# Graph attention on one core: the edge stage worked in pairs of units, with sums kept in four PSUM banks

## The reference

```
row, col = src, dst                                  # 212500 edges, 12500 nodes
xn = layernorm(h) * ln_w + ln_b                      # h = relu(layernorm(x)), H = 256
w_phys = (silu(rbf @ w1 + b1) @ w2 + b2) * cutoff[:, None]
msg_phys = xn[col] * w_phys
Q, K, V = xn @ wq + bq, xn @ wk + bk, xn @ wv + bv   # 8 heads of 32
scores = sum(Q[row] * K[col], -1) / sqrt(32) * cutoff[:, None]
attn = softmax(scores, axis=1)                       # over the 8 heads of an edge
combined = msg_phys + gate * (attn[..., None] * V[col])
aggr = segment_sum(combined, row)
out = x + h + aggr @ wo + bo
```

## Time and profile before

| | us |
|---|---|
| three executions, median | 6338.68 (6328.91 to 6351.49) |
| the profiled execution, its own time | 6347.99 |
| its span, first to last instruction | 6346.2 |
| PE busy | 5686.0 (90% of the span) |
| PEld busy | 4356.2 (69%) |
| DVE busy | 4708.3 (74%) |
| ACT busy | 3227.2 (51%) |
| POOL busy | 3783.6 (60%) |

### The profile page before, as it was taken

How to read it: one execution, slowest core, us unless ns; L and a number is a source line. 1 busy time by engine, 2 the same in 40 slices (tenths; PEclk the granted TensorE clock), 3 DMA queues, 4 the chain that set the end, 5 groups by cost and what they waited for, 6 DMA issues and landing times. The chain is left out here.

```text
span 6346.2 us, 114713 instructions
## 1 busy us (share of the span) xinstructions
PE 5686.0 (90%) x25995; PEld 4356.2 (69%) x25996; DVE 4708.3 (74%) x12728; ACT 3227.2 (51%) x12136; POOL 3783.6 (60%) x3580
## 2 busy tenths in 40 slices
PE   3689988889888888898799999999999999999999
PEld 3456655556555555565587787878888787788887
DVE  8588865555544444322599999999999999999995
ACT  4223322232322323222477777777777777777774
POOL 1466766666666566656666666666666666666660
PEclk9789999999999999998899999999999999999999
DMA  8433344334334433333698888988988888889835
GB/s 299 145 104 116 130 143 139 106 134 145 117 117 140 139 101 134 132 103 121 244 339 300 299 298 297 313 299 295 312 297 296 291 298 300 297 301 300 300 103 169
DMA packets 488176, 1350.47 MB, mean 213 GB/s; under 512 B 89614, under 2 KB 167222, under 8 KB 484858
## 3 DMA queue, kind: packets, MB, share of 16 engines
q0 software_dynamic: 230240, 900.22, 41.8%
q1 hardware_dynamic: 206904, 371.04, 18.1%
q10 hardware_dynamic: 50850, 77.03, 3.4%
HBM read 1074.68 MB, written 350.21 MB: 225 GB/s over the span
## 5 line engine op out<-in xcount | busy, mean ns | idle before, releaser
L937 POOL DMA_INDIRECT ukvx<-kvx_table,udst x1856 | 1946.4, 1049 | 1182.1 <-issue 534.8
L325 POOL DMA_INDIRECT records<-rows,slot_i x1660 | 1752.3, 1056 | 1141.6 <-DVE rows L574 522.6
L652 PE MATMUL w_ps<-w2s,hid 128*128 128x256 f32 x6656 | 1633.6, 400 | 226.7 <-DVE rows L574 203.3
L652 PEld LDWEIGHTS w_ps<-w2s,hid 128*128 128x128 f32 x6656 | 1289.6, 200 | 596.6 <-DVE rows L574 238.8
L758 ACT ACTIVATE hid<-hid_ps,b1t 128x512 f32<-128x512 f32 x832 | 525.7, 683 | 1888.7 <-PE hid_ps L641 964.3
L574 DVE TENSOR_TENSOR rows<-w_ps,b2b 128x512 f32<-128x512 f32 x832 | 569.0, 686 | 1196.4 <-remote 523.3
L1029 PE MATMUL uq_ps<-aggr,uonehotT 128*128 (+1 forms) x3712 | 1015.4, 396 | 95.0 <-issue 73.3
L1038 PE MATMUL ag_ps<-ukvx,uonehot_cut 128*128 128x256 f32 x3712 | 955.3, 380 | 0.1
L1041 PE MATMUL ag_ps<-ukvx,uonehot 128*128 128x256 f32 x3712 | 954.3, 380 | 0.0
L1038 PEld LDWEIGHTS ag_ps<-ukvx,uonehot_cut 128*128 128x128 f32 x3712 | 706.9, 190 | 97.0 <-issue 0.5
L1041 PEld LDWEIGHTS ag_ps<-ukvx,uonehot 128*128 128x128 f32 x3712 | 706.8, 190 | 96.5
(11 more groups left out here) (166 smaller groups left out, 6160.2 us busy)
## 6 DMA issues: line engine op xcount, KB each, us to landing
urec<-records SPq DMA_DIRECT2D x928, 260.0 KB
rbf_in<-in_edge_attr SPq DMA_DIRECT2D x207, 256.0 KB
kvx_table<-kvx ACTq DMA_DIRECT2D x10, 3456.0 KB
ukvx<-kvx_table,udst POOLq DMA_INDIRECT x1856
records<-rows,slot_i POOLq DMA_INDIRECT x1661
records<-kvx SPq DMA_DIRECT2D x1, 25480.0 KB
fbase<-x_plus_h SPq DMA_DIRECT2D x14, 896.0 KB, 7.1
out<-fout SPq DMA_DIRECT2D x13, 896.0 KB, 4.9
```

The costliest lines, as they stand in the source:

```text
L325: pool.indirect_dma_start(recs, bass.IndirectOffsetOnAxis(ap=slot_i[:, q, t:t + 1], axis=0), rows[:, q, t, :], None).then_inc(scattered[q] ...
L652: m = pe.matmul(w_ps[j % 2][:, h, :], hid[:, k % 2, c, h, j * P:(j + 1) * P], w2s[:, c, :], start=(h == 0 and c == 0), stop=(c == 1), skip ...
L937: pool.indirect_dma_start(kvx[:, k, j, :], None, table, bass.IndirectOffsetOnAxis(ap=dst_i[:, k, j:j + 1], axis=0), bounds_check=NPAD - 1, ...
```

## The change

- The unit of work in `edges` becomes a pair of units: four tiles, a ring of four pairs (RP) instead of eight units, 464 pairs. Instructions that took two tiles now take four where a PSUM bank allows it; the product of queries and keys stays in two halves.
- The sum stays in PSUM. Bucket b is summed in bank b mod 4. Ahead of each unit's sum PE writes zeros, with a bf16 product (L1070), into the bank after the one of the unit before. The identity product is gone. ACT copies the bank of bucket b - 2 to SBUF for both units of a pair (L1011), into the place that held that bucket's queries, and no longer writes zeros.
- The one-hots are made and transposed three pairs ahead, at the end of a pair's turn on DVE and PE. The gather goes three pairs ahead; its place is free when the pair before the present one has been summed.
- The normalised weights go to SBUF (`uattn`). The cutoff is copied out of the records (`ucut`, L974), so that SP waits for `phys_done`, `onehot_ready` and `dst_ready` before it loads a place anew.
- PE sums one pair behind instead of three units: filter products (`filtered`) between the two halves of the next pair's queries, the attention products (`attended`) after them.
- The first load of queries ahead of the records takes 7 buckets and not 28; the other 21 follow the first four loads of records. DVE instead of POOL clears the ring at the start.

PE, in the edge loop, one unit before. `uq_ps` are the queries, `ag_ps` the sums; the rows named ISA and REGISTER_ALU are instructions of PE's sequencer that put together addresses and counts.

The diff, cut to what the prediction speaks of:

```diff
-LAG = 3
+RP = DEPTH // 2
+BANKS = 4
...
+        GATHER_AHEAD, TURN_AHEAD, EVACUATE_AHEAD, QUERY_AHEAD, SUM_BEHIND, KEEP_BEHIND = 3, 3, 2, 1, 1, 1
...
-            sp.dma_start(aggr[:, QLAG:QLAG + QAHEAD * QC, :], q_v[:, 0:QAHEAD * QC, :]).then_inc(q_in, 16)
+            sp.dma_start(aggr[:, QLAG:QLAG + QC, :], q_v[:, 0:QC, :]).then_inc(q_in, 16)
...
+                    sp.wait_ge(s["phys_done"], v - (RP - 1))
+                    sp.wait_ge(s["onehot_ready"], v - (RP - 1))
+                    sp.wait_ge(s["dst_ready"], v - (RP - 1))
...
+                    pool.wait_ge(s["ag_done"], v - (RP - 1))
+                pool.wait_ge(s["dst_ready"], v + 1)
+                pool.sem_inc(s["dst_waited"], 1)
+                for j in range(4):
...
+            def keep(v, bucket, half):
+                if half == 0:
+                    if isinstance(v, int) and v == 0:
+                        act.wait_ge(s["zeroed"], 2)
+                    else:
+                        act.wait_ge(s["ag_done"], v)
+                        act.wait_ge(s["kept"], v)
+                else:
+                    act.wait_ge(s["half_kept"], v + 1)
+                act.activation(aggr[:, bass.ds(bucket + half, 1), :].rearrange("p a f -> p (a f)"), bank(bucket + (2 + half)),
+                               ACT.Copy).then_inc(s["half_kept" if half == 0 else "kept"], 1)
...
+            def turn(v, k, i, first):
+                pe.wait_ge(s["onehot_ready"], v + 1)
+                if not (isinstance(v, int) and v == 0):
+                    pe.wait_ge(s["ohT_ready"], v)
+                for j in range(4):
+                    m = pe.transpose(turn_ps[:, j, :], ohb[:, k, j, :], ident_bf[:])
+                m.then_inc(s["turned"], 1)
...
+                if half == 0:
+                    pe.wait_ge(s["ohT_ready"], v + 1)
+                    if not (first and k < 2):
+                        pe.wait_ge(s["qka_done"], v - 1)
+                elif not (isinstance(v, int) and v == 0):
+                    pe.wait_ge(s["qkb_done"], v)
...
+            def filtered(v, k, before, buckets):
+                if not (isinstance(v, int) and v == 0):
+                    pe.wait_ge(s["kept"], v)
+                pe.wait_ge(s["cut_ready"], v + 1)
+                pe.wait_ge(s["phys_done"], v + 1)
+                pe.sem_inc(s["ag_waited"], 1)
+                for a, former in enumerate((before, buckets[0])):
+                    pe.matmul(ag_ps[:, 0, 0:H] if former is None else bank(former + 1), zeros_bf[:, 0:P], zeros_bf[:], start=True, stop=True, skip_group_check=True)
+                    to = bank(buckets[a])
+                    for j in range(2):
+                        pe.matmul(to, ohc[:, k, 2 * a + j, :], kvx[:, k, 2 * a + j, 2 * H:3 * H], start=False, stop=False, skip_group_check=True)
+
+            def attended(v, k, buckets):
+                to = [bank(b) for b in buckets]
+                pe.wait_ge(s["wide_ready"], v + 1)
+                pe.wait_ge(s["av_done"], v + 1)
+                for a in range(2):
+                    for j in range(2):
+                        m = pe.matmul(to[a], oh[:, k, 2 * a + j, :], kvx[:, k, 2 * a + j, H:2 * H], start=False, stop=(j == 1), skip_group_check=True)
+                m.then_inc(s["ag_done"], 1)
...
+                if k == 0:
+                    near[:] = load_table(mybir.EngineType.PE, 1 if first else i * (2 * RP) + 1, 2 * RP + 5)
...
+                asked, summed = near[2 * k + 5:2 * k + 7], near[2 * k + 1:2 * k + 3]
+                asking, summing = not (last and k + QUERY_AHEAD >= RP), not (first and k < SUM_BEHIND)
+                if asking:
+                    query(v + 1, (k + 1) % RP, 0, asked[0], first and k + 1 < RP)
+                if summing:
+                    filtered(v - 1, (k - 1) % RP, None if first and k == 1 else near[2 * k], summed)
+                if asking:
+                    query(v + 1, (k + 1) % RP, 1, asked[1], first and k + 1 < RP)
+                if summing:
+                    attended(v - 1, (k - 1) % RP, summed)
+                ahead(turn, TURN_AHEAD, v, k, i, first, last)
...
+            def pair(v, k, i, first, last):
+                query_key(v, k, i, first, 0)
+                query_key(v, k, i, first, 1)
+                physical(v, k, i, first)
+                score(v, k, i, first)
+                behind(invert, 1, v, k, i, first)
+                weigh(v, k, i, first)
+                behind(normalise, 1, v, k, i, first)
+                maximum(v, k, i, first)
+                behind(attend, 1, v, k, i, first)
+                ahead(select, TURN_AHEAD, v, k, i, first, last)
```

More of the change, by code:

```diff
@@ L1008, in _, with pair @@
-            turns(act, unit)
-            _, rest = nc.values_load_multi_w_load_instructions(lagged_bucket[0:1, UNITS:UNITS + DEPTH], engines=[mybir.EngineType.Activation], min_val=0, max_val=BUCKETS - 1,
-                        skip_runtime_bounds_check_because="the table was clamped to the last bucket where it was written")
-            for n in range(LAG):
-                keep(UNITS - LAG + n, DEPTH - LAG + n, rest[n])
+            first_of = [None] * RP
+            def pair(v, k, i, first, last):
+                if k == 0 and not first:
+                    first_of[:] = load_table(mybir.EngineType.Activation, i * (2 * RP) + 2, 2 * RP)[0::2]
+                elif k == KEEP_BEHIND and first:
+                    first_of[KEEP_BEHIND:] = load_table(mybir.EngineType.Activation, 4, 2 * RP - 2)[0::2]
+                ahead(evacuate, EVACUATE_AHEAD, v, k, i, first, last)
+                widen(v, k, i, first)
+                if not (first and k < KEEP_BEHIND):
+                    keep(v - KEEP_BEHIND, first_of[k], 0)
+                ahead(destinations, GATHER_AHEAD, v, k, i, first, last)
+                if not (first and k < KEEP_BEHIND):
+                    keep(v - KEEP_BEHIND, first_of[k], 1)
+                exponent(v, k, i, first)
@@ L1014, in _ @@
+            turns(act, pair)
+            bucket = load_table(mybir.EngineType.Activation, UNITS + 2, 1)[0]
+            for half in range(2):
+                keep(PAIRS - 1, bucket, half)
+            act.wait_ge(s["ag_done"], PAIRS)
+            act.activation(aggr[:, QLAG + BUCKETS - 1, :], ag_ps[:, (BUCKETS - 1) % BANKS, 0:H], ACT.Copy).then_inc(s["kept"], 1)
         @block.tensor
         def _(pe):
-            def turn(u, k, i, first):
-                pe.wait_ge(s["onehot_ready"], u + 1)
-                if not (first and k < 2):
-                    pe.wait_ge(s["ohT_ready"], u - 1)
-                for j in range(2):
-                    m = pe.transpose(turn_ps[k % 2][:, j, :], ohb[:, k, j, :], ident_bf[:])
-                m.then_inc(s["turned"], 1)
@@ L1050, in _ @@
             pe.wait_ge(q_in, 16)
-            query(0, 0, 0, True)
-            near = [None] * (DEPTH + LAG + 1)
-            def unit(u, k, i, first, last):
-                ahead(turn, TURN_AHEAD, u, k, i, first, last)
-                if k == 0:
-                    _, near[:] = nc.values_load_multi_w_load_instructions(
-                        lagged_bucket[0:1, 0:DEPTH + LAG + 1] if first else lagged_bucket[0:1, bass.ds(u, DEPTH + LAG + 1)],
-                        engines=[mybir.EngineType.PE], min_val=0, max_val=BUCKETS - 1,
-                        skip_runtime_bounds_check_because="the table was clamped to the last bucket where it was written")
-                if not (last and k + 1 >= DEPTH):
-                    query(u + 1, (k + 1) % DEPTH, near[k + LAG + 1], first and k + 1 < DEPTH)
-                if not (first and k < LAG):
-                    aggregate(u - LAG, (k - LAG) % DEPTH, near[k], first)
@@ L1075, in _ @@
[L1075 to L1076 removed]
+            turns(pe, pair, asked_for)
+            end = load_table(mybir.EngineType.PE, UNITS + 1, 3)
+            filtered(PAIRS - 1, RP - 1, end[0], end[1:3])
+            attended(PAIRS - 1, RP - 1, end[1:3])
         @block.vector
         def _(dve):
[L1080 to L1083 removed]
+            dve.memset(zeros_bf[:], 0.0).then_inc(s["zeroed"], 1)
@@ L1131, in attend @@
[L1131 to L1136 removed]
+                dve.wait_ge(s["recip_done"], v + 1)
```

344 lines of the change are left out of this document (155 added, 189 removed).

## The result

The changed kernel takes 6543.75 us (median of 4 runs, 6536.3 to 6586.23) and the kernel before, on the same chip, 6333.8 us (median of 4, 6293.0 to 6351.49). The ratio is 1.0355, 95% interval 1.0288 to 1.0422: **slower by 3.6%**, where 6050 us, faster, was forecast. The profiled execution took 6536.3 us with a span of 6534.5, 188 us more than the span of before.

A forecast was written before the change was run, and what follows sets the result against it. PE and DVE were taken to bound the edge stage together. PE's 5.79 us times 1.055 gives 6.11 us a pair against 6.734, over 464 pairs 289 us gained: 6050 us, forecast's own range 5930 to 6110, whole range 5930 to 6190.

The forecast's parts named there:

- "At nothing", PE's register and address work: PE's sequencer in the edge loop: work grows from 6 to 13 instructions a pair, hidden by running ahead, at no cost.
- Rival B: DVE-to-PE hand-over: PE waits at `av_done`, then pays the bucket-number load in full; 6.38 us a pair, 6175 us; chance 0.15.
- The ring of gathers: Loop from gathers through DVE to attended products in the edge stage: 17.32 us for three pairs, 5.77 us a pair.
- Landing: Time from the last gather's start until DVE goes on, in the edge stage: 6.65 us, lower bound 2.1 us.
- rival C: Gathers land too late, so slower: break-even at 9.5 us from last gather's start; at 11 us, 6565 us; chance 0.08.
- The factor of 1.055: Edge-stage period over the slowest engine's own time, kept from before: 5.79 us becomes 6.11 us a pair.
- PE, 5.79 us: PE's own work for a pair in the edge stage: 5.79 us against 6.38, by the bounds 5.56 to 5.88.
- DVE, 5.68 us a pair: DVE's own work for a pair in the edge stage, with doubled instructions: 5.68 us against 6.30.
- the 5.3 us: DVE's pair if each of seven saved instructions also saved a fixed 157 ns; weighed and turned down.
- The start of the stage: Start of the edge stage, with fewer early loads and DVE clearing the ring: 8 us gained to 10 lost, taken as 0.
- A, transfers: DMA transfers bind the edge stage: at least 6.19 us a pair, 252 us gained, 6087 us; chance 0.15.
- D, nothing gained: PE, DVE and the gather loop lock in step, every wait passed on, at a factor of 1.16; chance 0.04.

The follow-up runs named there:

- aligned, quick chip: Changed kernel with PE's and ACT's loads of bucket numbers begun at a multiple of 8, on a chip where before took 5730.63 us: 5725.26 us, 0.9992.
- aligned, first group: Changed kernel with PE's and ACT's loads of bucket numbers begun at a multiple of 8, where before took 6340.94 us: 6385.94 us, 1.0054.
- the release in halves: Changed kernel with loads begun at a multiple of 8, a pair's first two gathers starting after half the sums; quick chip: 5627.66 us, 0.9819.
- the smaller gathers: Changed kernel with loads begun at a multiple of 8, each gather fetching only the keys, a third of a row: 5550.76 us, 0.9686.
- the half release run: Changed kernel with loads begun at a multiple of 8 and gather buffers released in halves, where before took 6323.48 us: 6339.64 us, 1.0027.
- the one with a third of each row: Changed kernel with loads begun at a multiple of 8, buffers released in halves and gathers fetching only keys: 6233.23 us, 0.9987.

## Why the prediction was wrong, point by point

**"At nothing", PE's register and address work: this step failed first.** It rested on the sequencer running ahead of the array; the read of bucket numbers was carried on at before's 0.95 us a turn, inside the factor. The read became 3.11 us, for a reason that I had not looked at: the number that it starts at. Rival B named the right place, but priced it at 1.06 us a turn where 2.69 us was measured on the quick chip. With alignment alone put right, 312 us of 6037 go there, and 160 to 190 on the slower ones.
The Trainium skill ("Runtime: NRT & Kernel Launch", Instruction fetch mechanics) gives about 200 ns a register for such loads, even in bulk; it says so where it speaks of register loads that the runtime puts in. The misaligned reads, of a table in SBUF, agree with it (0.22 to 0.24 us a number); the aligned ones don't (0.07, and 0.10 for ACT's ten). By that rate before's read of 12 numbers would be an estimated 2.4 us, and it takes 0.85.

**The ring of gathers: its length was wrong, and in other terms than I had doubted.** Means over pairs 200 to 399, from starts in the trace, in us for a loop of three pairs:

| part of the loop | predicted | aligned, quick chip | aligned, first group | after, first chip |
|---|---|---|---|---|
| sums taken to first gather | 0 | 1.07 | 1.97 | 1.55 |
| first to last gather | 3.93 | 4.28 | 4.37 | 4.40 |
| last gather to DVE's start | 6.65 | 6.01 | 6.14 | 6.43 |
| DVE, first half to values | 5.02 | 5.18 | 5.50 | 5.89 |
| values to attended products | 0 | 0.41 | 0.52 | 1.27 |
| attended products | 1.72 | 1.96 | 2.09 | 2.01 |
| sum | 17.32 | 18.91 | 20.59 | 21.55 |

Such a sum is three periods whatever binds, so the column alone proves nothing; the release in halves and the smaller gathers do, on quick chips (98 and 175 us under the aligned kernel's 5725.26). Landing, the term I doubted and on which rival C hung, was taken too high, 6.65 for 6.01 to 6.43 even with DVE's own lateness in it. What I had left out were the two hand-overs, at 0 each: from PE to POOL, which takes 0.95 us at the very least and 1.07 on average where no signal is late, and from DVE to PE. On the quick chip the terms come to 0.53 us a pair more than predicted, 6.30 instead of 5.77, or 246 us in 464 pairs.

**The factor of 1.055** was read as engines of equal length locking in step. On the quick chip before runs at 3.19 us, a factor of 1.00, with the same instructions. What the slower chip's trace has and the quick one's hasn't are PE's late signals. Their waits stood among those of POOL and ACT of before, 4500 to 5500 us, and were left unused:
```profile
POOL ukvx L937 <- remote: 134.8, 74, 2.2
ACT aggr L987 <- remote: 129.0, 72, 3.1
```
The quick chip's trace has no such wait in mid-stage. In my sum the wait of 57 us in 1000 was put down to the read of bucket numbers and the identity product. The sizes agreed, but the cause can't be those two alone: on the quick chip the same code hides both. That the late signals make the whole factor was not tested.

**PE, 5.79 us, and DVE, 5.68 us a pair: right.** The shortest twentieth of the periods of the aligned kernel is 5.70 us, on both chips. DVE's turns without any wait take 5.69 us at least and 5.75 in the median (141 of them, quick chip, 3300 to 5000 us), so the 5.3 us that the prediction weighed and turned down are out (6.30 less seven times 0.157 makes 5.2, not 5.3). DVE's doubled instructions start 1.13 us apart (5006.78 and 5007.91) for 1.11 taken; a zeros product lets the next start after 0.11 us (5005.58 and 5005.69 in the half release run), the lower of the values expected, which makes PE 5.67. **The work that was to go has gone**: no identity product, no wait of PE for ACT's copy.

**The start of the stage** took nothing extra: DVE multiplies its first queries and keys at 3073.41, 23 us earlier than before, and on the quick chip at 2643.2 where before did at 2642.9. With 0.44 us a pair lost in 464 pairs, 204 us, less the 23, that gives 181 of the 188 us between the profiled executions.

**The rivals.** A, transfers: no; their share fell to 0.82, and half release moves 328 GB/s where the aligned kernel moves 317. B: right place, far too cheap. C: the sign, and a loop over its break-even of 20.2 us (21.55), but by the read and the hand-overs, with a landing under 9.5 us. D, nothing gained: that is what the aligned kernel gives (0.9992 and 1.0054 to 1.0082), on the quick chip by the ring and not by equals in step; on the slower ones half release gives 35 us and the rest stays open. My 0.08 for C stood on landing alone; a loop of six parts, two of them set to nothing, should have had more.

**The version that comes out best** is the change with aligned reads and release in halves: 0.9819 and 0.9834 on two quick chips, 1.0027 on a slower one, against 1.0355 to 1.0538 for the change as it stands.

## What to carry to other kernels

When an edit touches the index at which an engine's sequencer reads a table, look at the start as well as the length: here 13 numbers from one place past a multiple of eight cost 3.11 us and 16 from a multiple of eight 1.11. From such a start 8, 12 and 16 numbers took 0.07 us each, but ten took as long as eight and two at 0.22, so a surplus that fills up four numbers looks cheap and a remainder dear, an estimate from these four lengths; whether a start at a multiple of four would do was not tried. When buffers are turned into a ring, write its loop with every hand-over in it, each at the shortest one that the trace shows and never at zero, and release a buffer in pieces if its consumer works in pieces. A period over the slowest engine's own time is no constant to be carried on: look for what ends the waits, those of unnamed events among them, before a factor is kept.

## What was not expected of the hardware

- Chips differ by 10% on one and the same kernel (before: 5730.63, 5734.39, 6240.84, 6323.48, 6333.8 and 6340.94 us). Of the 622 us between two profiled spans (5723.8 and 6346.2), 454 lie ahead of the edge stage: DVE starts on its first keys at 2642.9 on one and 3096.5 on the other.
- Late signals of PE on the slower ones, with waits of about 1.8 us behind them in step with the program: in before, in the changed kernel and in the one with a third of each row, but hardly any in before with its table moved by one number. What causes them stays open; so does whether before's gaps ahead of the bucket numbers come from them.
- Behind the pause of PE of 2.6 us shown above the granted clock was 0.63 over the next 4.5 us. Not every such pause has that behind it: over 4500 to 5500 us a stretch at half clock follows 21 of the 27 pauses of 2.5 us and more, on the quick chip over 3900 to 4900 us 5 of 27, and in before with its table moved, with pauses of up to 3.3 us, the mean was 1.00. In before, with pauses of up to 1.7 us ahead of the queries, the mid-stage had 1.00. The pauses' effect was not measured apart from their cause.
